# Two 3x3 convolutions with group norm on one Trainium2 core: a reworked chain ahead of the first convolution, weight loads on two queues, zero matmuls in idle PE, constants loaded later

## The reference

```python
x = x + _L0_conv_ref(_gn(x), w_fft_real, w_fft_imag, rot_w, rot_b, bn_gamma, bn_beta)
x = x + _L1_conv_ref(_gn(x), weight)          # a fixed 3x3 convolution

# in _L0_conv_ref
z = jnp.einsum('bchw,oc->bohw', x, rot_w) + rot_b[None, :, None, None]
z = (z - mu) * lax.rsqrt(var + BN_EPS)        # mu, var over images and pixels
z = z * bn_gamma[None, :, None, None] + bn_beta[None, :, None, None]
angle = jnp.tanh(jnp.sum(jnp.mean(z, axis=(2, 3)), axis=1, keepdims=True)) * (jnp.pi / 4)
phase = jnp.exp(-2j * jnp.pi * (jnp.cos(angle)[:, 0][:, None, None, None] * fsum))
rotated = jnp.fft.ifftn(w_fft[None] * phase[:, None, None], axes=(-3, -2, -1)).real
w2d = rotated[:, :, :, mid, :, :]             # 3x3 taps of each image
out = lax.conv_general_dilated(xg, gw, padding=[(1, 1), (1, 1)], feature_group_count=B, ...)
```

## Time and profile before

| | |
|---|---|
| median of 3 runs | 1771.41 us (1770.29 to 1773.91) |
| the profiled execution | 1773.2 us, its span 1771.4 us |
| PE busy | 1650.0 us (93%) |
| DVE busy | 1388.7 us (78%) |
| ACT busy | 1173.0 us (66%) |
| POOL busy | 120.3 us (7%) |
| moved by DMA | 411.56 MB, 232 GB/s over the span |
| mean granted PE clock | 0.979 |

### The profile page before, as it was taken

How to read it: one execution, slowest core, us unless ns; L and a number is a source line. 1 busy time by engine, 2 the same in 40 slices (tenths; PEclk the granted TensorE clock), 3 DMA queues, 4 the chain that set the end, 5 groups by cost and what they waited for, 6 DMA issues and landing times.

```text
span 1771.4 us, 65148 instructions
## 1 busy us (share of the span) xinstructions
PE 1650.0 (93%) x29275; PEld 1269.7 (72%) x29275; DVE 1388.7 (78%) x2249; ACT 1173.0 (66%) x1056; POOL 120.3 (7%) x347
## 2 busy tenths in 40 slices
PE   5888888678789999999999999999999999999999
PEld 5777878444456667998688768866786678666755
DVE  6988999779978888878888888787878888878600
ACT  6888878569756666666666666666666666666444
POOL 0000000030010010002000200020002000100100
PEclk9999999879999999999999999999999999999999
DMA  9999999455446665666666666566666666665245
GB/s 385 421 422 422 422 422 422 186 163 168 137 137 201 202 204 187 225 194 200 211 205 204 190 216 214 187 206 210 200 194 208 209 205 196 208 199 202 109 196 203
DMA packets 101782, 411.56 MB, mean 232 GB/s; under 512 B 16883, under 2 KB 19496, under 8 KB 85160
## 3 DMA queue, kind: packets, MB, share of 16 engines
q1 hardware_dynamic: 100168, 405.71, 65.1%
q10 hardware_dynamic: 576, 2.10, 0.4%
q0 software_dynamic: 800, 0.15, 0.1%
HBM read 271.82 MB, written 136.07 MB: 230 GB/s over the span
## 4 chain that ended last, share of the span: by engine, by line
PE 69%; DVE 14%; DMA 6%; issue 6%; ACT 4%; SPq 1%; DVEq 0%; POOL 0%; ACTq 0%; POOLq 0%
PE ps L430 36%; PE ps L423 32%; DVE x L667 6%; DMA x<-x_pix 6%; DVE x L883 2%; DVE nat L717 2%; ACT x L539 1%; DVE stats L921 1%; ACT x L497 1%; ACT nat L524 1%; ACT x L537 1%; PE ps L373 1%; SPq L260 0%; PE ps L374 0%; DVE x L717 0%
## 5 line engine op out<-in xcount | busy, mean ns | idle before, releaser
L430 PE MATMUL ps<-x,wc 64*64 64x512 f16 (+2 forms) x12585 | 1161.1, 375 | 3.3 <-POOL x L647 3.3
L423 PE MATMUL ps<-nat,wc 64*64 64x512 f16 (+1 forms) x11784 | 1139.3, 378 | 24.0 <-DVE x L883 13.6
L430 PEld LDWEIGHTS ps<-x,wc 64*64 64x64 f16 x12585 | 679.2, 107 | 172.1 <-POOL x L647 4.4
L423 PEld LDWEIGHTS ps<-nat,wc 64*64 64x64 f16 x11784 | 657.6, 107 | 194.6 <-issue 44.7
L524 ACT ACTIVATE nat<-xin,gnp 128x1024 f16<-128x1024 f32 (+1 forms) x249 | 283.2, 1139 | 294.2 <-PE ps L423 289.7
L883 DVE SCALAR_TENSOR_TENSOR x<-ps,gnp,x 128x1024 f16<-128x1024 f32 (+1 forms) x264 | 333.1, 1262 | 31.4 <-ACT x L539 23.3
L554 ACT ACTIVATE outb<-ps,bias 128x1024 f32<-128x1024 f32 (+1 forms) x264 | 289.4, 1096 | 75.0 <-PE ps L430 58.3
L543 ACT ACTIVATE x<-ps,gnp 128x1024 f16<-128x1024 f32 (+1 forms) x227 | 248.4, 1094 | 114.7 <-DVE stats L921 114.3
L717 DVE SCALAR_TENSOR_TENSOR nat<-xin,gnp,nat 128x1024 f16<-128x1024 f32 (+1 forms) x249 | 313.3, 1259 | 2.0 <-ACT nat L524 1.9
L373 PE MATMUL ps<-x 128*128 128x129 f16 x2048 | 258.4, 227 | 59.2 <-DVE x L667 59.0
L667 DVE SCALAR_TENSOR_TENSOR x<-x 128x2048 bf16<-128x2048 f32 x128 | 284.2, 2288 | 17.6 <-ACT x L497 16.0
(11 more groups left out here) (134 smaller groups left out, 374.6 us busy)
## 6 DMA issues: line engine op xcount, KB each, us to landing
x<-x_pix SPq DMA_DIRECT2D x128, 1024.0 KB, 13.5
out<-outb SPq DMA_DIRECT2D x256, 512.0 KB, 4.3
xin<-x_tiles SPq DMA_DIRECT2D x252, 512.0 KB, 3.8
xin<-x_tiles ACTq DMA_DIRECT2D x4, 512.0 KB, 5.2
xin<-x_tiles SPq DMA_DIRECT2D x8, 192.5 KB, 2.4
out<-outb SPq DMA_DIRECT2D x8, 192.5 KB, 3.4
w<-taps_scratch SPq DMA_DIRECT2D x64, 8.0 KB, 1.9
w<-taps_scratch SPq DMA_DIRECT2D x28, 16.0 KB, 2.7
```

The costliest lines, as they stand in the source:

```text
L423: return nc.tensor.matmul(ps[64 * kind:64 * kind + 64, bank, 0:w], lhs, planes[rows, xhl, a:a + w], start=first, stop=last)
L430: ins = nc.tensor.matmul(ps[64 * kind:64 * kind + 64, bank, done:done + part], lhs, x1[rows, xhl, z:z + part], start=first and done == 0, ...
```

## The change

- SP issues no constants before x. ACT issues four of them (`first`, `rw`, `smallp`, `wfs`; some 290 KB) when the first x load has landed; `cst` and `w1band` (450 KB) follow on SP after the stream and the first four chunks. DVE waits for the four, PE for the two others only after the folds.
- The five steps between images become four independent ones: both accumulators are masked separately and the column sums scaled separately. The fold takes both, with `fold` and `fold2` = 2 `fold`, accumulating in PSUM. The fold and reduce of images 0 to 3 is done after image 5; the loop over pairs of images is split there.
- `zpad` is set at the very beginning.
- `load_weights` of image 0: six loads by SP, six by ACT, none by POOL. Chunks 4 to 7 of x are issued by SP behind its six. ACT does two `hi0`, its weight loads, then the rest; DVE two `lo0`, `weights0`, then the rest.
- For later images SP issues the twelve weight loads in threes, at chunks 8 to 11.
- After `Z_S` PE does seven matmuls of zeros.
- In image 1 no chunk's sums are ACT's.
- PE waits for the moments of image 0 one bank later (L474), as for the images 1 to 6.

```diff
 def by_act(b, n):
-    return n < TAIL0 and (n % 5 != 0 if b == 0 else 0 < n < 3)
+    if b == 0:
+        return n < TAIL0 and n % 5 != 0
+    return b > 1 and 0 < n < 3
...
         def load_weights(eng, b, groups, signal):
             for half, r in groups:
-                for ci in range(2):
-                    g = ((half * 2 + r) * 2 + ci) * C
-                    for rows, m in (((r, 4), 0),) if half == 0 else (((2 + r, 2), 0), ((r, 2), 128)):
...
+                g = (half * 2 + r) * 2 * C
+                for row, count, m in ((r, 4, 0),) if half == 0 else ((2 + r, 2, 0), (r, 2, 128)):
+                    for ci in range(2):
...
         def _(sp):
-            for dst, src in ((cst[:, :], consts), (first, firsts), (rw[:, :], rotw), (smallp[:, :], small),
-                             (wfs, wf), (w132[:, :], w1band)):
-                sp.dma_start(dst, src).then_inc(const_in, 16)
...
             for g in range(NX):
                 load_x(g)
+            for dst, src in ((cst[:, :], consts), (w132[:, :], w1band)):
+                sp.dma_start(dst, src).then_inc(late_in, 16)
...
-            load_weights(sp, 0, ((1, 0), (1, 1)), w_in)
+            load_weights(sp, 0, ((0, 0), (1, 0)), w_in)
+            for g in range(NX, 2 * NX):
+                load_x(g)
...
-                if n == 8 and b < B - 1:
-                    sp.wait_ge(w0_ready, b + 1)
-                    sp.wait_ge(taps_rest, 16 * 3 * (B - 1))
-                    load_weights(sp, b + 1, ((0, 0), (0, 1), (1, 0), (1, 1)), w_in)
+                if 8 <= n < 12 and b < B - 1:
+                    if n == 8:
+                        sp.wait_ge(w0_ready, b + 1)
+                        sp.wait_ge(taps_rest, 16 * 3 * (B - 1))
+                    load_weights(sp, b + 1, (divmod(n - 8, 2),), w_in)
...
+            def fold(h):
+                pe.wait_ge(a_mask, 4 * (4 * h + 4 + 2))
+                for f, name in enumerate(("fold", "fold2")):
+                    m = nc.tensor.matmul(ps[0:C, 6 + h, 0:512], c(name),
+                                         gmask[:, f, 4 * h:4 * h + 4, :].rearrange("p b q -> p (b q)"),
+                                         start=f == 0, stop=f == 1)
+                m.then_inc(folded, 1)
+            with pe.Fori(0, B // 2 - 1) as bb:
+                gram_pair(bb)
+            pe.wait_ge(const_in, 16 * 4)
+            fold(0)
+            with pe.Fori(B // 2 - 1, B // 2) as bb:
+                gram_pair(bb)
...
-            pe.wait_ge(const_in, 16 * 6)
-            pe.wait_ge(zve, Z_SUMS)
-            for h in range(2):
-                mm(ps[0:C, 2 + h, 0:512], c("fold"), gmask[:, 4 * h:4 * h + 4, :].rearrange("p b q -> p (b q)"), False)
-            mm(ps[0:C, 4, 0:B], c("fold"), colsum)
+            fold(1)
+            for f in range(2):
+                m = nc.tensor.matmul(ps[0:C, 4, 0:B], c("fold"), colsum[:, f, :], start=f == 0, stop=f == 1)
+            m.then_inc(folded, 1)
+            pe.wait_ge(late_in, 16 * 2)
...
             pe.wait_ge(zve, Z_S)
+            for _ in range(WARM):
+                nc.tensor.matmul(ps[:, 6, 0:P + 1], zerof[:, 0:P], zerof[:, 0:P + 1], start=True, stop=True)
...
-                        if job in means and (q == 0 if means[job] in ALONE else ends):
+                        if job in means and (q == 0 if means[job] == B - 1 else ends):
...
         def _(act):
+            act.wait_ge(a_in[0], 16)
+            for dst, src in ((first, firsts), (rw[:, :], rotw), (smallp[:, :], small), (wfs, wf)):
+                act.dma_start(dst, src).then_inc(const_in, 16)
...
-            for g in range(NX):
+            for g in range(2):
                 hi0(g)
-            for g in range(NX, 2 * NX):
-                act.wait_ge(lo0_ready, g - NX + 1)
-                act.dma_start(xin[:, g % NX, :], x_tiles[0, :, g * CH:(g + 1) * CH]).then_inc(x_in[g % NX], 16)
+            act.wait_ge(zdma, 16 * 4)
+            load_weights(act, 0, ((0, 1), (1, 1)), w_in)
+            for g in range(2, NX):
+                hi0(g)
...
             pool.wait_ge(zdma, 16 * 4)
-            load_weights(pool, 0, ((0, 0), (0, 1)), w_soft)
...
+            V.memset(zpad, 0.0).then_inc(zve, 1)
...
-                    V.tensor_copy(gtmp, ps[:, h, 0:P]).then_inc(a_part, 1)
-                    V.tensor_copy(gcol[:, 0:1], ps[:, h, P:P + 1]).then_inc(a_part, 1)
-                    ve.wait_ge(a_part, 3 * b + 2)
-                    V.scalar_tensor_tensor(gtmp, ps[:, 2 + h, 0:P], 2.0, gtmp, ALU.mult, ALU.add).then_inc(a_part, 1)
-                    V.tensor_tensor(colsum[:, bass.ds(b, 1)], ps[:, 2 + h, P:P + 1], gcol[:, 0:1], ALU.add)
-                    hold(ve, a_part, 3 * b + 3)
-                    V.tensor_tensor(gmask[:, bass.ds(b, 1), :].rearrange("p b q -> p (b q)"), gtmp,
-                                    c("mask_g"), ALU.mult).then_inc(a_mask, 1)
+                    for f in range(2):
+                        V.tensor_tensor(gmask[:, f, bass.ds(b, 1), :].rearrange("p b q -> p (b q)"), ps[:, 2 * f + h, 0:P],
+                                        c("mask_g"), ALU.mult).then_inc(a_mask, 1)
+                        V.tensor_scalar(colsum[:, f, bass.ds(b, 1)], ps[:, 2 * f + h, P:P + 1], AS, None, ALU.mult
+                                        ).then_inc(a_mask, 1)
...
+            with ve.Fori(0, B // 2 - 1) as bb:
+                halves_pair(bb)
+            fold_sums(0).then_inc(zve, 1)
+            with ve.Fori(B // 2 - 1, B // 2) as bb:
+                halves_pair(bb)
...
-            for g in range(NX):
+            for g in range(2):
                 lo0(g)
             for part in range(4):
                 weights0(0, part)
+            for g in range(2, NX):
+                lo0(g)
```

More of the change, by code:

```diff
@@ L46 @@
 ALONE = (0, B - 1)
+WARM = 7
 YS = 16.0
@@ L86 @@
 _COLS = [("gm", 128), ("id0", 256), ("id1", 256), ("pmask", 2), ("row0", 1), ("rown", 1)]
-_FIRST = [("mask_g", 128), ("fold", 16), ("rep", 128), ("pair", 16), ("id16", 16),
+_FIRST = [("mask_g", 128), ("fold", 16), ("fold2", 16), ("rep", 128), ("pair", 16), ("id16", 16),
           ("ones", 128), ("u", 9), ("v", 9), ("trig", 4), ("quarter", 1), ("image", 8)]
@@ L174, in conv_program @@
         at_[0] = RCOLS // 2
-        gmask = early(B * P).rearrange("p (b q) -> p b q", b=B)
-        colsum, gcol, gtmp = early(B), early(1), early(P)
+        gmask = early(2 * B * P).rearrange("p (f b q) -> p f b q", f=2, b=B)
+        colsum = early(2 * B).rearrange("p (f b) -> p f b", f=2)
         gram = early(B * C, C).rearrange("p (b c) -> p b c", b=B)
@@ L256, in load_weights @@
             for half, r in groups:
-                for ci in range(2):
-                    g = ((half * 2 + r) * 2 + ci) * C
-                    for rows, m in (((r, 4), 0),) if half == 0 else (((2 + r, 2), 0), ((r, 2), 128)):
-                        eng.dma_start(w32[g:g + C, m:m + 64 * rows[1]].rearrange("c (a m) -> c a m", m=64),
-                                      taps[b, :, rows[0]:rows[0] + rows[1], ci:ci + 4, :].rearrange(
-                                          "c a q o -> c a (q o)")).then_inc(signal, 16)
+                g = (half * 2 + r) * 2 * C
+                for row, count, m in ((r, 4, 0),) if half == 0 else ((2 + r, 2, 0), (r, 2, 128)):
+                    for ci in range(2):
+                        at_ = g + ci * C
+                        eng.dma_start(w32[at_:at_ + C, m:m + 64 * count].rearrange("c (a m) -> c a m", m=64),
+                                      taps[b, :, row:row + count, ci:ci + 4, :].rearrange("c a q o -> c a (q o)")
+                                      ).then_inc(signal, 16)
         def reads(n):
@@ L358, in _, with gram_pair @@
             pe.wait_ge(a_zero, 1)
-            with pe.Fori(0, B // 2) as bb:
+            def gram_pair(bb):
                 for h in range(2):
@@ L655, in _, with halves_pair @@
             ve.sem_inc(a_lo, ASLOTS)
-            ve.sem_inc(a_mask, 2)
+            ve.sem_inc(a_mask, 8)
+            V.memset(zpad, 0.0).then_inc(zve, 1)
             V.memset(ahi[:, :, :, P:P + 1], 1.0)
             V.memset(zerof, 0.0).then_inc(a_zero, 1)
-            ve.wait_ge(const_in, 16 * 6)
-            with ve.Fori(0, B // 2) as bb:
+            ve.wait_ge(const_in, 16 * 4)
+            def halves_pair(bb):
                 for h in range(2):
@@ L725, in lo0 @@
                 ins.then_inc(lo0_ready, 1)
-            count = [0]
+            count = [2]
             def go(ins):
@@ L756, in at @@
                 assert k == n, (k, n)
-            link(V.memset(zpad, 0.0))
-            ve.wait_ge(a_mask, B + 2)
-            at(link(V.tensor_scalar(colsum, colsum, AS, None, ALU.mult)), Z_SUMS)
-            after_pe()
-            for hh in range(2):
-                n = go(V.tensor_reduce(gram[:, 4 * hh:4 * hh + 4, :],
-                                       ps[0:C, 2 + hh, :].rearrange("p (b k c) -> p b c k", b=4, k=8),
-                                       AX.X, ALU.add))
```

(8 more changed lines are left out.)

24 lines of the change are left out of this document (13 added, 11 removed).

## The result

The changed kernel takes 1764.98 us (median of 6 runs, 1763.55 to 1765.67), the kernel before beside it 1771.63 (6 runs): a ratio of 0.9959, 95% interval 0.9949 to 0.9969, so 7.3 us less (5.5 to 9.0). The forecast was 1763.0. The profiled execution of the changed kernel took 1764.9 us with a span of 1763.1, that of before 1773.2 with 1771.4. These two are 8.3 us apart and the forecast sum was 8.4; it is the medians that lie closer together, by 6.7. That the one pair meets the sum is chance, as the experiments show.

A forecast was written before the change was run, and what follows sets the result against it. Bounds: x transfers, a dependent chain, VectorE in the first image, then PE from about 508 us (1260 us, unchanged). Terms sum to 8.4 us: profiled 1773.2 to 1764.8, less 1.8 for the median: 1763.0; range 1759.5 to 1767.5.

The forecast's parts named there:

- Stream: First pass over x, 0 to 330.6 us: first x load sooner without constants ahead; -1.9 us, bounds -0.7 to -3.2.
- rival D: Start of stream: constants starve behind x loads, VectorE starts late; 1769.5 us, or 1793 at worst; chance 0.05.
- Rival C: Stream: the 1.2 us slip ahead of load 8 goes with the constants; 1.3 us more, 1761.7; chance 0.09.
- Chain: Small dependent steps after the stream, 330.6 to 356.4 us: independent steps and one reduce fewer; -1.9, bounds -1.5 to -2.1.
- Clock of the fold: Fold after the stream: PE idles less, so it runs at 2.4 GHz, not 1.2; -1.7 us, bounds 0 to -1.8.
- Start of the convolution: From 356.4 to 374.8 us: weights 2.7 us earlier, 1.6 lost to later x loads; -1.1, bounds +0.7 to -2.5.
- new waits at pads 6 and 8: Start of the convolution: VectorE newly waits on x loads 6 and 8; if missing, this part gives more.
- seven zero matmuls: After Z_S: they buy nothing and cost nothing, ending before the weights are there; 0 us.
- Rival B: Start of the convolution: weights gain only two issues, 0.9 us; part +0.7 instead of -1.1, total 1764.8; chance 0.12.
- First image: From 375 to 508 us: weight loads in threes, -1.6 us; image 1's changed sums, -0.2 us.
- split burst: First image: weight loads in threes remove VectorE's 1.75 us wait for a late x load; -1.6, bounds -1.0 to -1.75.
- sums in image 1: Image 1, chunks 1 and 2: VectorE does the sums instead of ScalarE; -0.2 us, bounds +0.5 to -0.6.

The follow-up runs named there:

- r1: Changed kernel, but ScalarE issues the four constants at once, not after the first x load has landed: 1762.75 us, ratio 0.9948.
- r11: Changed kernel with constants issued at once, lo0 of chunk 2 ahead of the weights, and 20 zero matmuls instead of 7: 1762.18 us, ratio 0.9951.
- r2: Changed kernel, but the four constants are issued by SP at the head of its queue, ahead of the x loads: 1763.77 us.
- r8: The kernel before, unchanged, traced a second time: 1770.51 us, span 1768.7.
- r4: Changed kernel, but PE also waits for four VectorE memsets ahead of fold(1), so it idles longer: 1765.91 us.
- r9: Changed kernel, image 0's weight loads again eight by SP, four by GpSimd; ACT issues x loads 4 to 7; four lo0 ahead of weights: 1766.79 us, ratio 0.9971.
- r3: Changed kernel without the zero matmuls after Z_S: 1764.26 us.
- r5: Changed kernel, but image 0's weight loads go eight by SP, four by GpSimd; x loads 4 to 7 stay on SP: 1764.53 us.
- r6: Changed kernel, but later images' twelve weight loads go in a row at chunk 8, and ScalarE takes image 1's sums of chunks 1 and 2 again: 1767.58 us.

## Why the prediction was right, and where not

Right in sign and range: 1765.0 lies inside 1759.5 to 1767.5, and from the averaging matmul of image 0 to the end the time changed by 0.6 us only. The forecast was 2.0 too low. In its own order:

**Stream (-1.9; it was -0.9).** The first issue (1.41 for 1.5) and the first landing (about 6.3 for 6.5) are right, and r1 and r11 give the full 1.9. The step that failed is "the mask for VectorE lands about 3 us after its issue, near 11.5". The prediction names no row for it; the nearest that it had, 2.2 to 4.6 us, are of weight loads of 8 or 16 KB beside at most four x loads. Behind eight x loads in SP's queue the four constants took 10.9 us from the last issue. This is rival D, of which the prediction said that it decides at a start after about 20 us: VectorE started at 19.1 and lost 1.0 us, so that point lay too late as well. Two extremes had been worked out, the constants' share of the bytes (0.7 us) and all eight x loads ahead of them (8 x 2.49 = 20); the truth lay between. The page DMA: Bandwidth & Descriptors of the Trainium skill (Queues, rings and completion order), cited against D, also says that an engine drains a whole packet of several descriptors of one ring before it turns to the next. That the small queue would get its share in bytes does not follow from it, and the trace, with 10.9 us where that share would be 0.7, agrees. Rival C's slip ahead of load 8 is 1.5 us in r2 and r11 (1.3 in before) and 0.6 in r1 and in r8, the kernel before: it does not go by the constants.

**Chain (-1.9; it was -2.0).** 24.19 to 22.18 with both folds at clock 1.00. The twelve traces of the changed kernel and its variants lie at 21.8 to 22.2, but for r4 at 23.4.

**Clock of the fold (-1.7; nothing that can be counted on).** The mechanism as stated, a shorter idleness keeps the clock up, is not what decides: with 2.0 us (r4, r8) the clock was up as well. The changed fold ran at 1.00 in all twelve traces, the fold before in one of two, so some of the term may be real; how much, two traces of before don't say. And r8 shows an error in the sum. The forecast took 1.7 us out because the profiled execution had a slow fold, and took another 1.8 out because that execution lay above the median. That would be right if every execution of before had the slow fold. But it hadn't, and the slow fold is part of why this one lay high: r8, with a quick fold and a quick end, took 1770.5. So the same time was subtracted twice, in part at least; what the median execution of before has, no trace shows. Without the clock's term the forecast would have been 1764.7.

**Start of the convolution (-1.1; it was -1.9, and -1.2 in the first pair).** The weights are there 5.1 us after Z_S as forecast, and for the reason given (r9). The new waits at pads 6 and 8 came, 2.37 and 0.57 us. The term is mis-sized: before, the stage takes 18.48 in one trace and 19.19 in the other, and of the 1.9 us found r9 traces 1.0 to the x loads and the order of work, which is the part that the prediction had worked out; the cause of the other 0.9 stays open. The seven zero matmuls buy nothing, as forecast (r3). Rival B, the weights gaining two issues, falls with r5 and r9: the second queue gained not even those.

**First image (-1.6 and -0.2; it was -1.5 and -0.6).** The split burst is right within 0.2 us, against two traces of before and r6 (1.7). Of the sums in image 1 the best bound came true. The forecast set 0.9 us of delay against the 0.85 us wait of PE that it would cover. That wait (0.85 us at 502.19 in r6) is gone in every trace of the changed kernel. But one job earlier PE waits between 0 and 1.2 us in them (0.85 in the first, 0.19 in r6), so that it isn't shown what the delay cost; the stretch as a whole gives the 0.6, against before and against r6.

Sum: the clock 1.7 too much and the stream 1.0, the start 0.8 and the rest 0.5 too little, which leaves 1.4 of the 2.0; what remains is within what a median of six can tell. That errors of both signs nearly halved the miss is luck.

## What to carry to other kernels

If a sum starts from one profiled execution, a term that depends on the granted clock must be checked in a second trace of the same kernel, and if it isn't in every execution it must not be taken out again by the step from that execution to the median. A small load that an engine waits for goes out ahead of a saturated queue, not after its first landing: here some 0.3 MB sent from 6.3 us on arrived at 19.1, sent from 0.8 on it arrived at 10.6. And warming an engine up pays only if the work fills the time up to the first real instruction and the engine is what is late next; of the two edits at the start, one alone gave 0.6 us and the other nothing that shows, and both 1.9.

## What the runs showed of the hardware

- Behind the same gap the clock of PE falls in one execution and not in another: 3.45 and 1.91 us for one fold, 1.7 us at the end of the kernel. Two such places are worth up to 3.2 us, and the end of the stream moves by up to 1.5 us (328.91 to 330.38 in nine traces), while the executions of the kernel before beside the changed one lie between 1768.6 and 1773.9.
- Four loads of together some 0.3 MB on ACT's queue, under x loads of 1 MB on SP's at 422 GB/s, took 10.9 us from the last issue to landing, 7.9 when issued beside the first x loads (r11). The last weight load of image 0, issued until 353.97 with x loads only behind it (from 354.00 on), landed by 356.56, 2.6 us later.
- Behind seven matmuls of zeros (3.20 us) the clock rose in one trace, 0.3 us before they were over, and it was at 0.50 again when PE's next work came 3.83 us later; in another it stayed at 0.50.
